# Two token buffers that change places by batch, eight queries in the feed-forward, four values in the second cross attention

## The reference, cut to what matters

```python
x = ln(x + windowed_causal_attention(x, Wq, Wk, Wv, Wo))   # a: 16 heads of 32; each window of 512 queries
                                                           #    sees keys 0 .. its own place only
x = ln(x + cross_attention(x, ctx, mask, ...))             # b
x = ln(x + x @ base_w.T + lora_mixture(x))                 # c
x = ln(x + flow_attention(x, ...))                         # d
x = ln(x + softmax(x @ ctx.T * 512**-0.5) @ ctx)           # e: causal mask, 64 context rows
x = ln(x + bit_linear(silu(conv3(bit_linear(x, w1))), w2)) # f: int8 activations, ternary weights
```

## Time and profile before

| | |
|---|---|
| median of three runs | 2606.01 us |
| profiled execution: its own time, its span | 2608.17 us, 2606.3 us |
| PE busy | 2350.9 us, 90% |
| DVE busy | 1591.2 us, 61% |
| ACT busy | 1247.5 us, 48% |
| mean granted TensorE clock | 0.979 |

### The profile page before, as it was taken

The page is one execution under the profiler, slowest core; times in us unless marked ns, Lnnn a source line. Parts: engine busy times, 40 slices in busy tenths (PEclk is TensorE's granted clock), DMA queues, the critical chain, the costliest instruction groups (busy, mean ns, idle before and its releaser), DMA issues.

```text
span 2606.3 us, 37060 instructions
## 1 busy us (share of the span) xinstructions
PE 2350.9 (90%) x13000; PEld 1303.8 (50%) x13000; DVE 1591.2 (61%) x3101; ACT 1247.5 (48%) x2870; POOL 691.7 (27%) x989
## 2 busy tenths in 40 slices
PE   7989999989988999998898999999899899999866
PEld 3655544545565544454556554435455655444443
DVE  4664643569866462457977655155797746516698
ACT  5763212259675321227967431222886723122396
POOL 0002140037401232013820213201480031310366
PEclk9999999999999999999999999999999999999988
DMA  8001010010210200001030101001003010100000
GB/s 300 18 11 49 24 45 33 0 49 1 87 50 10 72 29 17 32 1 49 9 128 2 55 26 29 32 17 49 1 9 128 2 58 23 29 17 1 0 1 33
DMA packets 58988, 99.43 MB, mean 38 GB/s; under 512 B 13364, under 2 KB 13748, under 8 KB 58296
## 3 DMA queue, kind: packets, MB, share of 16 engines
q1 hardware_dynamic: 58808, 97.06, 11.3%
HBM read 88.66 MB, written 8.39 MB: 37 GB/s over the span
## 4 chain that ended last, share of the span: by engine, by line
PE 61%; DVE 18%; ACT 14%; issue 4%; POOL 2%; DMA 0%; ACTq 0%; DVEq 0%; POOLq 0%; SPq 0%
PE psum L398 20%; PE psum L392 13%; ACT prob L810 6%; PE psum L424 4%; PE psum L483 3%; DVE neg_max L1106 3%; PE psum L549 2%; DVE f_a L1113 2%; PE psum L451 2%; PE psum L791 2%; DVE bn L1056 2%; DVE f_top L1392 2%; PE psum L620 1%; ACT f_z L1008 1%; PE psum L763 1%
## 5 line engine op out<-in xcount | busy, mean ns | idle before, releaser
L398 PE MATMUL psum<-weights,mixed 128*128 128x512 f32 x768 | 341.2, 595 | 0.0
L392 PE MATMUL psum<-xT,weights 128*128 128x512 f32 x768 | 334.5, 593 | 0.0
L810 ACT ACTIVATE prob<-psum,neg_max 128x128 f32<-128x128 f32 (+3 forms) x512 | 265.0, 543 | 109.3 <-DVE neg_max L1106 109.3
L1430 POOL TENSOR_SCALAR var<-stats 128x1 f32<-128x1 f32 x192 | 63.8, 332 | 797.2 <-DVE stats L1057 797.1
L1106 DVE TENSOR_REDUCE neg_max<-psum 128x1 f32<-128x128 f32 (+3 forms) x512 | 217.5, 483 | 81.2 <-PE psum L488 46.5
L846 ACT COPY xT<-psum 128x512 f32<-128x512 f32 x128 | 70.3, 590 | 367.4 <-PE psum L451 367.4
L1087 DVE TENSOR_TENSOR x<-psum,x 128x512 f32<-128x512 f32 x128 | 88.4, 691 | 244.8 <-PE psum L398 172.7
L398 PE MATMUL psum<-weights,xT 128*128 128x512 f32 x512 | 232.9, 598 | 2.4 <-DVE recip L1295 1.6
L1443 POOL TENSOR_TENSOR f_a<-f_a,f_z 128x256 f32<-128x256 f32 x256 | 204.5, 809 | 113.8 <-DVE f_a L1113 113.8
L392 PEld LDWEIGHTS psum<-xT,weights 128*128 128x128 f32 x768 | 144.0, 190 | 172.4 <-issue 172.2
L398 PEld LDWEIGHTS psum<-weights,mixed 128*128 128x128 f32 x768 | 141.6, 190 | 167.5 <-issue 166.7
(11 more groups left out here) (246 smaller groups left out, 4193.1 us busy)
## 6 DMA issues: line engine op xcount, KB each, us to landing
xT<-in_xT SPq DMA_DIRECT2D x8, 1024.0 KB, 6.4
x<-in_x SPq DMA_DIRECT2D x8, 1024.0 KB, 8.9
out<-x SPq DMA_DIRECT2D x16, 512.0 KB, 2.8
weights<-in_a_k SPq DMA_DIRECT2D x4, 1024.0 KB, 5.3
weights<-in_a_q SPq DMA_DIRECT2D x4, 1024.0 KB, 5.1
weights<-in_a_v SPq DMA_DIRECT2D x4, 1024.0 KB, 5.0
w1f<-in_w SPq DMA_DIRECT2D x4, 1024.0 KB, 14.9
w2f<-in_w SPq DMA_DIRECT2D x4, 1024.0 KB, 17.3
```

The costliest lines, as they stand in the source:

```text
L392: last = mm(bank[:, 0:n], weights[weight][:, c, heads(g)], rhs(c), start=(c == 0), stop=(c == C - 1))
L398: last = mm(bank, lhsT(c), weights[weight][:, c, :], start=(c == 0), stop=(stop and c == C - 1))
L810: last = run(sb["prob"][:, slot, o:o + keys], bank[:, o:o + keys], ACT.Exp, bias=sb["neg_max"][:, n, qc, j:j + 1], accum_out=sb["a_sum"][: ...
```

## The change

The buffers `xT` and `mixed` become `tok0` and `tok1`. In an even batch the tokens are in `tok0` and the mixed heads in `tok1`; in an odd batch the other way round. The next batch's tokens are loaded into the buffer of mixed heads, one window after `d_out 3` and one after `d_out 7`. The eight queries are kept where later the mixed heads of the same group and window are written. `a_ring` no longer carries projections.

The diff, cut to its core; the other hunks replace `xT[...]` and `sb["mixed"]` by `of_window`, `of_tile`, `turned_tokens()` and `mixed()`.

```diff
-FIRST_PROJECTIONS = [("a_key", 0), ("a_query", 0), ("a_value", 0), ("a_key", 1), ("a_value", 1), ("a_query", 2),
-                     ("a_value", 2), ("a_query", 1), ("a_value", 3), ("a_key", 2), ("a_query", 3), ("a_key", 3)]
+EARLY_PROJECTIONS = [("a_value", t) for t in range(WT)]
+FIRST_PROJECTIONS = [("a_query", n) for n in range(W * C)] + [("a_key", g) for g in range(C)]
...
-           ("a_query", 3), ("p_round", 6), ("p_ternary", 5), ("p_round", 7), ("p_ternary", 6), ("p_ternary", 7), ("p_cast",)]
+           ("a_query", 3), ("p_round", 6), ("a_query", 4), ("p_ternary", 5), ("a_query", 5), ("p_round", 7), ("a_query", 6), ("p_ternary", 6),
+           ("a_query", 7), ("p_ternary", 7), ("p_cast",)]
...
-        if i < W * C - Q_SLOTS:
-            steps.append(("a_query", Q_SLOTS + i))
...
+    following = b < B - 1
...
+    steps += [("x_ahead", 0)] * following
...
-              ("d_out", 6), ("transpose", 4, 4), ("e_gather", 0), ("d_out", 7), ("transpose", 4, 5), ("e_turn", 0), ("e_out", 0, 0),
-              ("transpose", 4, 6), ("transpose", 4, 7), ("e_out", 0, 1)]
-    if b < B - 1:
-        steps += [("weight_ahead", 0)]
-    steps += [("e_score", 1)] + [("x_ahead",)] * (b < B - 1) + [("e_norm", t) for t in range(WT)]
-    steps += [("e_gather", 1), ("e_turn", 1), ("f_round", 0), ("e_out", 1, 0)] + [("f_turn", t) for t in range(WT)] + [("f_unit", 0)]
+              ("d_out", 6), ("transpose", 4, 4), ("e_gather", 0), ("d_out", 7), ("transpose", 4, 5)]
+    steps += [("x_ahead", 1), ("weight_ahead", 0)] * following
+    early = [[("next", ("a_half", *step, half)) for half in range(2)] * following for step in EARLY_PROJECTIONS]
+    steps += [("e_turn", 0), ("e_out", 0, 0), ("transpose", 4, 6), ("transpose", 4, 7), ("e_out", 0, 1)]
+    steps += [("e_score", 1), *early[0][:1]] + [("e_norm", t) for t in range(WT)] + [("e_gather", 1), *early[0][1:], ("e_turn", 1), *early[1][:1]]
+    steps += [("f_round", 0), ("e_out", 1, 0), *early[1][1:], *early[2], *early[3]] + [("f_turn", t) for t in range(WT)] + [("f_unit", 0)]
...
+    def turned_tokens():
+        return sb[f"tok{now[0] % 2}"]
+
+    def mixed():
+        return sb[f"tok{(now[0] + 1) % 2}"]
...
     def query(n):
-        return sb["a_q"][:, n, :] if n < Q_SLOTS else sb["a_q_late"][:, n - Q_SLOTS, :]
-
-    def query_ring(n):
-        return act_ring if n < Q_SLOTS else a_ring
+        return mixed()[:, n % W, n // W, :]
...
-                    if name == ("a_query", Q_SLOTS) and now[0] > 0:
-                        pe.wait_ge(q["f_out_taken"], at("f_out_taken", 0))
-                    bank = ring.claim(pe, name)
+                    bank = act_ring.claim(pe, name)
...
+                    if i == 1 and now[0] > 0:
+                        pe.wait_ge(q["f_out_taken"], at("f_out_taken", 0))
...
                 elif kind == "x_ahead":
-                    written(sp, ("e_score", 1))
-                    load_turned(sp, dram["xT"][now[0] + 1], sb, q)
+                    w, = arg
+                    written(sp, ("d_out", WT * w + WT - 1))
+                    load_turned(sp, dram["xT"][now[0] + 1], mixed(), w, q)
```

More of the change, by code:

```diff
@@ L259, in weight_rows, with load_turned @@
     return dram[WEIGHTS[i]].rearrange("(c p) n -> p c n", p=P)
[L262 to L266, removed]
+def load_turned(sp, xT, tok, w, done):
+    sp.dma_start(tok[:, w, :, :], xT.rearrange("(c p) n -> p c n", p=P)[:, :, D * w:D * w + D]).then_inc(done[f"ahead_loaded{w}"], 16)
 def ffn_chunk(sb, n):
@@ L297, in sequence @@
     b_heads = (banks[6], banks[7])
[L298 removed]
+    x, ident, ones = sb["x"], sb["ident"], sb["ones"]
     a_heads = banks[6]
@@ L404, in out_rows @@
                     bank = dve_ring.claim(pe, (f"{'abcdef'[stage]}_out", w * WT + t))
-                    rows(bank, lambda c: sb["mixed"][:, w, c, heads(t)], weight).then_inc(dve_ring.filled, 1)
+                    rows(bank, lambda c: mixed()[:, w, c, heads(t)], weight).then_inc(dve_ring.filled, 1)
             def a_project(name, chunks):
                 kind, n = name
-                ring = query_ring(n) if kind == "a_query" else act_ring
                 g, w = divmod(n, W) if kind == "a_query" else (n, 0)
@@ L540, in _ @@
                     xT_ready(pe, 1, WT * w + WT - 1)
-                    project(act_ring.claim(pe, step), "b_q", g, lambda c: xT[:, c, tokens(w)], D).then_inc(act_ring.filled, 1)
+                    project(act_ring.claim(pe, step), "b_q", g, lambda c: of_window(c, w), D).then_inc(act_ring.filled, 1)
                 elif kind == "b_score":
@@ L592, in _ @@
                     for c in range(C):
-                        last = mm(bank[HD * c:HD * c + HD, :], sb["c_rl"][:, c, :], xT[:, c, tokens(w)], start=True, stop=True)
+                        last = mm(bank[HD * c:HD * c + HD, :], sb["c_rl"][:, c, :], of_window(c, w), start=True, stop=True)
                     last.then_inc(act_ring.filled, 1)
@@ L612, in _ @@
                     weight_ready(pe, "c_w")
-                    rows(dve_ring.claim(pe, ("c_out", t)), lambda c: xT[:, c, heads(t)], "c_w", stop=False)
+                    rows(dve_ring.claim(pe, ("c_out", t)), lambda c: of_tile(c, t), "c_w", stop=False)
                 elif kind == "c_out":
@@ L631, in _ @@
                     weight_ready(pe, "d_v")
-                    rows(dve_ring.claim(pe, step), lambda c: xT[:, c, heads(t)], "d_v").then_inc(dve_ring.filled, 1)
+                    rows(dve_ring.claim(pe, step), lambda c: of_tile(c, t), "d_v").then_inc(dve_ring.filled, 1)
                 elif kind == "d_turn":
@@ L716, in _ @@
                             last = mm(bank[SK * half:SK * half + SK, :], sb["ctxT"][:, C // 2 * half + c, 0:SK],
-                                      xT[:, C // 2 * half + c, tokens(w)], start=(c == 0), stop=(c == C // 2 - 1))
+                                      of_window(C // 2 * half + c, w), start=(c == 0), stop=(c == C // 2 - 1))
                     last.then_inc(act_ring.filled, 1)
@@ L817, in a_projected @@
                 if kind == "a_query":
-                    run(query(n), query_ring(n).take(act, name), ACT.Copy, scale=SCALE).then_inc(query_ring(n).freed, 1)
+                    run(query(n), act_ring.take(act, name), ACT.Copy, scale=SCALE).then_inc(act_ring.freed, 1)
                 else:
@@ L845, in _ @@
                     bank = act_ring.take(act, step)
-                    copy(xT[:, :, heads(t)], bank.rearrange("p (c n) -> p c n", c=C)).then_inc(act_ring.freed, 1)
+                    copy(turned_tokens()[:, t // WT, :, heads(t % WT)], bank.rearrange("p (c n) -> p c n", c=C)).then_inc(act_ring.freed, 1)
                 elif kind == "p_abs":
@@ L931, in _ @@
                     t, = arg
-                    copy(sb["mixed"][:, t // C, t % C, :], act_ring.take(act, step)).then_inc(act_ring.freed, 1)
+                    copy(mixed()[:, t // C, t % C, :], act_ring.take(act, step)).then_inc(act_ring.freed, 1)
                 elif kind == "d_sums":
@@ L1634, in place @@
     put("x", [T, D])
-    put("xT", [C, S])
-    put("mixed", [W, C, D])
+    put("tok0", [W, C, D])
+    put("tok1", [W, C, D])
     put("recip", [D])
@@ L1655, in place @@
     put("a_k", [C, D])
-    put("a_q", [Q_SLOTS, D])
+    at[0] += C * D * 4
     put("a_v", [WT, D])
     put("turned", [TURN_SLOTS, D])
-    put("a_q_late", [W * C - Q_SLOTS, D])
     at[0] = room + 68 * 1024
```

28 lines of the change are left out of this document (15 added, 13 removed).

## The result

The changed kernel takes 2622.08 us (median of four runs, 2618.57 to 2624.69) against 2606.02 (median of four). The ratio is 1.0059, 95% interval 1.0042 to 1.0077: slower by 0.6%. The profiled execution took 2623.27 us with a span of 2621.5, which is 15.2 more than before. The forecast of 2612.5 had the sign and four tenths of the size (6.5 of 16.1 us); the time lies 1 us outside the range.

The account below looks back on a forecast made before the run. PE was busy 90%, but pace was judged stretch by stretch. Batch 0 +4.6, stage a -21.1, stage e +19.5 and clock +3.6 gave +6.6, taken as +6.5: 2606.01 to 2612.5 us, range 2601 to 2621.

Parts of the forecast that it names:

- What bounds each stretch: Start of stage a: PE paces groups with queries, the scores-to-exponentials loop paces bare groups; 7.03 us a batch gained.
- the price of a projection: Anywhere on PE: one projection costs 3.43 us, a half 1.72; four moved projections are 13.72 us.
- Warm-up: Before batch 0: four more queries delay group 1 by 10.74 us, groups 1 to 3 return 6.12; batch 0 4.6 worse.
- End of stage e: From `e_score 1` to the first hidden step: early values delay it 6.5 us a batch, 19.5 for three.
- These two halves cost nothing: Stage e, around `e_gather`: two value halves fit before the exponentials at 552.27, 6.09 us of work in 6.87.
- Only then come the turned rows: Stage e after `e_out`: turned rows wait behind five value halves, 8.58 us, ending at 564.73.
- Feed-forward and loads: Feed-forward keeps twelve projections in the same places, and earlier token and weight loads arrive in time: no cost.
- The clock: Start of stage a: without query 4 PE idles and the clock may drop, 0.9 us a batch, 3.6 for four.
- Clock stays up: Rival, start of stage a: turns and the scores' tail hold the clock; +3, 2609 us; chance 0.28.
- the feed-forward takes the delay back: Rival: DVE and ACT pace the feed-forward, absorbing stage e's delay; 2593 us, or 2603 with half; chance 0.12.
- the bare loop is not reached: Rival, groups 1 to 3: half of 6.12 lost, about 2625 us, or clock low through two groups, 2619; chance 0.12.

Follow-up runs that it names:

- PE kept busy: Changed kernel plus eleven small unread products behind group 0's scores in batches 1 to 3: 2610.72 us; also in waits of stages b to d: 2605.15 us.
- The experiment with two values: Against the changed kernel, two values instead of four in stage e, two queries kept among groups 0 and 1 of batches 1 to 3, old warm-up: 2597.52 us.
- the buffers alone: Kernel before with only the swapped token buffers and earlier token loads, all projections in their old order: 2606.25 us, ratio 0.9999.

## Why the prediction was wrong

Point by point, by its own steps:

- **What bounds each stretch, and the price of a projection: right.** Group 0 at 6.28 us, groups 2 and 3 at 5.74 and 5.75, and with PE kept busy 6.98 us a batch gained, forecast 7.03.
- **Warm-up: right.** +5.5 in the two traces, of which 0.7 stood before the added work already (queries 1 and 3 start at 48.61 instead of 47.88). That is scatter between executions: in the eight profiles with the old warm-up the first scores start between 55.71 and 56.60. The mean start of group 4, in those eight and in the four with the new warm-up and no fall in batch 0, differs by 4.9; forecast +4.6.
- **End of stage e: right, by step and size.** +6.70 a batch, forecast 6.5. "These two halves cost nothing" and "Only then come the turned rows" are both in the trace. The experiment with two values shows where the free part ends: four halves cost 0.46 us, the next four 6.24.
- **Feed-forward and loads: right.** Unchanged at 136.3; the buffers alone are neutral.
- **The clock: the step that failed.** "I take 0.9 a batch (a drop likely, not sure), 3.6 for four batches, since the scores are the nearest row." At that place it was about right: 1.0 to 1.1 us in batches 1 to 3, nothing in batch 0. But the term stopped there, and put the clock in all later stages at nothing without a reason. The clock also fell otherwise in stages c and d, whose instructions did not change, for +8.2 us in three batches. With 8.2 more and 0.3 to 0.6 less at the start of stage a, the forecast would have been 2620.3, within 2 us of the 2622.08 measured. I had in front of me that batch 0 and batches 1 to 3 of the kernel before differ there by 373.44 - 367.32 = 6.1 us with 3.4 us of column sums between them. The runs with PE kept busy give these sums 3.37 (369.52 - 366.15), so the other 2.7 us were the dear pattern in batch 0: a price read off the trace of before, had I asked what they were.

The runs show what makes it. Removing the fall behind group 0 took 3.0 us off group 1 and 7.7 off stages b to d of three batches in the profiled execution, while two of five executions gained only some 5 us; removing the falls in b to d brings both kernels to 366.15. That the falls can move with no edit at all shows in stages b to d of batch 0: with the same instructions they took 373.3 and 370.6 us in two profiles whose first scores stood 1.2 us apart. What stays open is why each batch returns to its own pattern after a shift, and why a fall at its start goes with the dear one.

Of the rivals, none was it. "Clock stays up" failed in batches 1 to 3, though in batch 0 of the profiled execution it did stay up; "the feed-forward takes the delay back" failed with 136.3 unchanged; "the bare loop is not reached" named a low clock through two groups, and got one, and groups 2 and 3 did reach the bare loop. That the 2622 us measured lie between its 2619 and 2625 is chance.

The Trainium skill, "TensorE: Matmul & The Clock Gate", section "HAM oscillation — how this bites in real kernels", tells of waits between bursts of matmuls after which each next burst starts cold. At the start of stage a the trace agrees in batches 1 to 3, with a wait of 2.67 us and the next burst at half clock. In batch 0 it does not: behind a wait of 1.73 us the burst took 1.14 us, at full clock, and behind the same wait in another profile 1.77. The prediction asked of that section only what the next burst costs. It did not ask how the falls further on would move.

## What to carry to other kernels

Moving work off an engine's critical stretch gives back only what stands above that stretch's own loop, and costs at the new place what its waits do not cover: count both by the same price and stop where the free waits end (here four of eight halves). Work that seems hidden in a wait of PE can also hold the clock up (here in a wait of 2.67 us); taking it away can cost in stages that the change does not touch. An edit that aims at the clock is judged by several executions, since one kernel can show two patterns (here 2608 to 2611 and 2616 to 2618 us). If the same stretch has two lengths in one trace, find out why before summing.

## What the runs showed of the hardware

- The granted clock fell from 2.4 to 1.2 GHz within 1.5 us of the end of waits of PE of 2.67 us (`prob`), 2.50 (`b_spread`), 2.48 (`c_gm`), 2.16 (`d_thin`) and 1.44 (`d_blk`). Behind the last, and behind one of 1.73 us, it fell in one trace and not in another with the same instructions.
- Eleven unread products of 2.55 us in the wait of 2.67 us kept the clock up there in three batches, and the profiled execution gained 10.7 us by it, 7.7 of them in later stages.
- The same stages with the same instructions took 366.15 us a batch (unread products in their waits), 367.3 or 370.0 us, and the difference is the granted clock in the stretches behind PE's waits: 1.00, 0.99 and 0.98 in the mean.
- 1.7 us of added work in batch 0 left its stages b to d 1.3 us shorter in the changed kernel and as long as they were in the kernel before, and left every later batch as it was, in both.
- Where the clock was held up by unread products in stages b to d, it could fall longer in the next place: `e_score 1` to the first hidden step took 17.28 instead of 16.36 us in three batches of the kernel before with twelve of them ahead of `e_turn 1`, and in two batches without those twelve.
